# A graph layer on one core: VectorE finishes a column block of the first pass behind the fifth group of one-hots instead of the second

## The reference, cut to what matters

```python
norm = dinv[edge_src] * dinv[edge_dst]
root = jnp.einsum('nf,kfg->nkg', x, root_w)
for t in range(num_layers):
    h = jnp.einsum('nf,kfg->nkg', x, init_w) if t == 0 else jnp.einsum('nkf,kfg->nkg', out, w)
    msg = h[edge_src] * norm[:, None, None]
    h = jax.ops.segment_sum(msg, edge_dst, num_segments=n)
    out = jax.nn.relu(h + root + b[None])
```

## Time and profile before

| | |
|---|---|
| median of 3 runs | 3698.93 us |
| profiled execution | 3698.62 us |
| its span | 3696.6 us |
| TensorE busy (matmul) | 3391.4 us, 92% |
| VectorE busy | 1307.2 us, 35% |
| ScalarE busy | 741.0 us, 20% |
| mean granted TensorE clock | 0.956 of full speed |

### The profile page before, as it was taken

The page is one execution under the profiler, slowest core; times in us unless marked ns, Lnnn a source line. Parts: engine busy times, 40 slices in busy tenths (PEclk is TensorE's granted clock), DMA queues, the critical chain, the costliest instruction groups (busy, mean ns, idle before and its releaser), DMA issues. The chain is left out here.

```text
span 3696.6 us, 50703 instructions
## 1 busy us (share of the span) xinstructions
PE 3391.4 (92%) x18037; PEld 1967.8 (53%) x18038; DVE 1307.2 (35%) x4668; ACT 741.0 (20%) x1510; POOL 254.4 (7%) x271
## 2 busy tenths in 40 slices
PE   6998999999999999996999999999999996539999
PEld 3574555555545555553555555555555545426776
DVE  7747777777711111110111112112111014434443
ACT  2445555555500000000000000000000002313333
POOL 3000000000000000000000000000000001442333
PEclk9997999999999999997999999999999998769999
DMA  7112332332289999999544449988889962317775
GB/s 190 64 46 77 138 125 102 147 148 107 110 319 301 307 304 314 307 304 286 166 154 149 149 145 327 302 284 282 287 284 298 304 221 81 117 64 242 249 235 200
DMA packets 262202, 761.01 MB, mean 206 GB/s; under 512 B 26067, under 2 KB 178571, under 8 KB 260022
## 3 DMA queue, kind: packets, MB, share of 16 engines
q1 hardware_dynamic: 171608, 616.10, 49.6%
q10 hardware_dynamic: 78814, 115.44, 12.0%
q0 software_dynamic: 11648, 27.76, 2.0%
HBM read 532.00 MB, written 239.86 MB: 209 GB/s over the span
## 5 line engine op out<-in xcount | busy, mean ns | idle before, releaser
L1505 PE MATMUL acc<-stage,split 128*128 128x448 f16 x5488 | 1045.9, 353 | 3.7 <-PEq L1456 3.7
L1505 PEld LDWEIGHTS acc<-stage,split 128*128 128x128 f16 x5488 | 537.8, 98 | 502.5 <-PEq L1456 4.0
L1505 PE MATMUL acc<-stage,other 128*128 128x448 f16 x4116 | 783.8, 353 | 0.0
L1211 PE MATMUL first_sum<-stage,other 128*128 128x448 f16 x2744 | 658.5, 357 | 0.2 <-ACT stage L1029 0.2
L1505 PEld LDWEIGHTS acc<-stage,other 128*128 128x128 f16 x4116 | 402.9, 98 | 377.7 <-issue 6.8
L1556 DVE TENSOR_TENSOR tmp<-acc,dinv_b 128x448 f32<-128x448 f32 x98 | 61.0, 623 | 1284.6 <-PE acc L1505 1284.6
L1029 ACT ACTIVATE stage<-group_ps 128x392 f16<-128x392 f32 x784 | 386.2, 497 | 341.4 <-PE group_ps L1200 337.9
L1075 DVE TENSOR_SCALAR place<-iota_col,rel 128x196 f16<-128x196 f16 x1568 | 349.1, 265 | 0.0
L1211 PEld LDWEIGHTS first_sum<-stage,other 128*128 128x128 f16 x2744 | 256.0, 99 | 143.8 <-issue 8.2
L1072 DVE TENSOR_TENSOR lanes<-iota_two,lane_two 128x256 f16<-128x256 f16 x784 | 225.9, 288 | 98.0 <-PE group_ps L1200 81.6
L1196 PE MATMUL group_ps<-place,lanes 128*128 128x196 f16 x784 | 200.9, 256 | 57.3 <-DVE place L1075 42.4
(11 more groups left out here) (338 smaller groups left out, 2593.6 us busy)
## 6 DMA issues: line engine op xcount, KB each, us to landing
stage<-adj_d SPq DMA_DIRECT2D x490, 784.0 KB, 4.3
adj_d<-stage SPq DMA_DIRECT2D x14, 5488.0 KB, 17.7
row_d<-blank ACTq DMA_DIRECT2D x20, 3340.5 KB
slot_weights<-pack_d SPq DMA_DIRECT2D x42, 898.0 KB, 5.1
part_d<-blank ACTq DMA_DIRECT2D x10, 3340.5 KB
slot_rows<-row_d SPq DMA_DIRECT2D x42, 393.0 KB
rin<-root_d SPq DMA_DIRECT2D x28, 448.0 KB, 8.5
slot_base<-row_d SPq DMA_DIRECT2D x21, 393.0 KB, 6.2
```

What stands on the lines that cost most here:

```text
L1211: m = mm(acc[b][k][:, 0:WIN], other[:, h, half, k * P:(k + 1) * P], stage[b][:, h, :], start=(h == 0 and half == 0), stop=(h == TILES - 1 ...
L1505: m = nc.tensor.matmul(acc[b][k][:, :], src[:, h, part, k * P:(k + 1) * P], ring[:, i, r, :], start=(h == 0 and part == 0), stop=(h == TIL ...
```

## The change

One line in VectorE's `quick()`: the call of `finished` goes from behind group 1 to behind group 4 of the same window, in the twelve windows 2 to 13. The two finishes behind the loop are as they were, and so are all other engines' programs.

```diff
                             group(pair, gp, (pair * PG + gp) % GPI)
                             if w == 0 and at in mixing:
                                 mixing[at]()
-                            if w >= 2 and at == 1:
+                            if w >= 2 and at == 4:
                                 finished((w - 2) // 2, w % 2)
                             if w >= 2 and at in hooks and hooks[at] < len(TAKEN[w % 2]):
                                 rows((w - 2) // 2, TAKEN[w % 2][hooks[at]])
```

## The result

The changed kernel takes 3665.5 us (median of four runs, 3658.7 to 3667.4) against 3698.1 us before in the same set of runs: a ratio of 0.9907 (95% interval 0.9891 to 0.9924), 32.6 us faster (28 to 40 by the interval). Predicted were 3666.6 us, within 3659 to 3685.

What follows compares the result with a forecast made beforehand. TensorE sets the build's pace, with twelve 3.34 us stalls for VectorE's one-hots. Shorter stalls (20.8 us) plus seven avoided clock falls (11.5) give 32.3 us: 3698.62 to 3666.3, plus 0.3 for the median, 3666.6 us, range 3659 to 3685.

Steps and rivals of the forecast that it cites:

- The lead: Build windows 2 to 13: with more groups in hand during VectorE's finish, TensorE starts group 5 1.73 us earlier, 20.8 us.
- The rival of the wait for the sum: Follow-up experiments' rival, no chance given: only VectorE's 1.57 us wait before the finish was recovered, so later places gain the same.
- The clock: Behind the twelve build stalls: shorter idle keeps TensorE at 2.4 GHz, so seven falls at 1.64 us go, 11.5 us.
- The first rival: Build stalls: TensorE's clock falls at all twelve, leaving 12.6 us gained, 3686.3 us; chance 8%.
- The sum: Whole kernel: 20.8 us from shorter stalls plus 11.5 from the clock, 32.3 us, kept to the end.
- the 0.14 us: Before group 2 in each window: TensorE's wait for ScalarE's copy of group 0, formerly hidden under the stall, 0.14 us.
- what is queued behind the finish: SyncE's loads and 5.5 MB store, three issues, go 0.74 us later; next needed most of a window away, costing nothing.

Runs made afterwards that it cites:

- the seventh group: The changed kernel with the finish moved on to stand behind the seventh group of the window; 3634.15 us against 3669.66 for the kernel before, ratio 0.9896.
- the doubled finish: The changed kernel with the six VectorE instructions of the finish done twice, same values rewritten; 3651.53 us against 3624.43 for the kernel before, ratio 1.0068.
- The filled stall: The kernel before with 15 unread matmuls put behind group 1 on TensorE in windows 2 to 13; 3607.90 us against 3624.43, ratio 0.9950.
- the halves: The changed kernel with the finish cut in two, behind the fifth and tenth groups; 3637.66 us against 3669.66 for the kernel before, ratio 0.9909.

## Why the prediction was right

**The lead.** Each step can be laid beside the rows of window 4 after. The finish begins right behind group 4 and takes 3.24 us (3.25 forecast); the first matmul of group 5 comes 483.88 - 483.27 = 0.61 us behind the start of its one-hots (0.61); the gain of the window is 1.73 us (1.73). The four other places and lengths of the finish that were tried give stalls of 2.17, 1.43, 0.57 and 4.75 us against 2.3, 1.5, 0.7 and 4.6 expected. The rival of the wait for the sum is refuted by the seventh group and by the doubled finish.

**The clock.** 11.5 of the 32.3 us were to come from seven falls that no longer happen. They don't, and the filled stall shows this term by itself, at an unchanged end of the stall: 11.8 us of build from window 2 on. For the length of idle that does no harm the prediction had a single row, of 1.57 us; that was enough at 1.25 us, and one group earlier, at 2.17 us, the whole term would have been missing. The first rival, twelve falls, had the right kind of mechanism for longer stalls (the doubled finish), not for 1.25 us. The Trainium skill (TensorE: Matmul & The Clock Gate, "What's actually happening") ties the slow clock to a long idle stretch, and the trace agrees for the change, in that stalls of 1.25 us brought no fall. It is no guide to where the danger begins: the clock also fell behind stalls of 1.98 and 2.17 us. Its warning on short idles between groups of matmuls ("A second HAM failure mode") is not borne out at 1.25 us in twelve windows.

**The sum.** 20.8 + 11.5 = 32.3 us were forecast; the build gained 32.1 and the runs 32.6. It was kept to the end as forecast. That the runs come within 0.3 us is luck, as their interval is 28 to 40 us; the build is the firmer number.

**What was off.** Two steps, without effect on the total. The first: the 0.14 us that TensorE would wait for ScalarE's copy are 0.26. The step of the semaphore to TensorE is 0.05 us, as taken (ScalarE's own behind group 0, which the prediction names for it, is 0.10: 488.03 - 487.93). But the three copies of the earlier trace rows do not share their 1.49 us evenly; the second of them, before and then after:

```profile
488.03 0.50 ACT L1029 ACTIVATE stage<-group_ps 128x392 f16<-128x392 f32 x1
```
```profile
479.51 0.50 ACT L1029 ACTIVATE stage<-group_ps 128x392 f16<-128x392 f32 x1
```

Before, it ends at 488.03 + 0.50 = 488.53 and not at 488.41. After, it ends at 480.00 (unrounded), and group 2 opens at 480.06. The start of group 5 does not depend on it.

The second: the step on what is queued behind the finish named three issues of SyncE and called their delay nothing. In even windows there is a fourth, the store of the rows, and its reader is not a window away. In the change it is issued at 484.62 and takes 5.7 us to land, and ScalarE's first high part starts at 492.30. That leaves 2.0 us; before the change it was 502.55 - 492.40 - 5.6 = 4.5. The prediction came out right because this cover was thinner than it believed but not used up, and that took some luck: a landing of 7.8 us, as two windows of the kernel with the finish two groups later have it, would have used it up in the change too (484.62 + 7.8 = 492.42).

## What to carry to other kernels

Work that blocks a feeding engine belongs where the engine it feeds has the most in hand: count that in microseconds of the fed engine's work, not in buffers (the two groups before carried no pass matmuls and were worth 0.8 us), and cut the work into pieces shorter than it. When a step that raises a semaphore is moved, list every issue behind that semaphore on every queue, in each kind of iteration, with when it lands and who reads it. If a shorter piece brings nothing, look for the next wait before giving it up: the halves looked like a failure until one store was moved.

## What the runs showed of the hardware that was not expected

The length of a stall did not decide alone whether TensorE's clock fell behind it. In these kernels it fell behind 7 of 12 stalls of 3.34 us, 7 of 12 of 2.17 us (with 0.26 us idle 0.9 us earlier), all 12 of 4.75 us, all 5 of 2.16 to 3.09 us in the halves, and both of 1.98 and 1.99 us near group 15. It did not fall behind the one of 1.65 us there, nor behind any of 12 of 1.43 us and 24 of 1.25 us. So the shortest stall with a fall was 1.98 us, and the longest that was seen twelve times without one 1.43 us; the single one of 1.65 us says little, since five of 3.34 us brought no fall either. Between the third and the fourth group the seven falls that went were worth 11.7 us of the build, more than the 8.9 us by which the stalls themselves became shorter. Why one stall of a kernel brings a fall and the next, alike in length, doesn't was not tested.

The kernel before took 3698, 3670 and 3624 us in three sets of runs; only within a set are the times comparable. Much of the difference lies in two waits of TensorE behind the build. The long stall of the later passes is 35.6 and 37.8 us in the two profiles of the first set and 5.9 to 9.5 us in the eight others. The wait of L1739 for ScalarE's L1781 in the last part is 41.2 us in both of the first set, 28.4 to 43.0 in the second and 16.1 to 16.7 in the third. Why, and where the rest lies, stays open.
